# A linear-attention and mixture-of-experts layer on one core: denominators placed directly behind the shared product, shared sums placed behind the reciprocals

## The reference, cut to what matters

```
xn  = layernorm(x)
Q, K, V = heads(xn @ wq.T + bq), heads(xn @ wk.T + bk), heads(xn @ wv.T + bv)   # 16 heads of 32
Q, K = elu(Q) + 1, elu(K) + 1
out = (Q @ (K^T V)) / (Q . sum(K) + 1e-8)          # linear attention, per head
att = out @ wo.T + bo
gate = xn @ W_gate + shared lora + expert loras * w    # up likewise; w from a top-2 router
hidden = silu(gate) * up                               # 1376 wide
ffn = hidden @ W_down + (hidden @ sA_down) @ sB_down / 8 + expert loras of down
result = x + att + ffn
```

## Time and profile before

| | |
|---|---|
| median of 3 runs | 667.39 us |
| the profiled execution's own time | 667.35 us |
| its span, first to last instruction | 665.6 us |
| TensorE busy | 656.5 us (99%) |
| VectorE busy | 376.3 us (57%) |
| ScalarE busy | 259.3 us (39%) |
| GpSimd busy | 127.3 us (19%) |
| granted TensorE clock, mean | 1.000 |

### The profile page before, as it was taken

How to read it: one execution, slowest core, us unless ns; L and a number is a source line. 1 busy time by engine, 2 the same in 40 slices (tenths; PEclk the granted TensorE clock), 3 DMA queues, 4 the chain that set the end, 5 groups by cost and what they waited for, 6 DMA issues and landing times.

```text
span 665.6 us, 10324 instructions
## 1 busy us (share of the span) xinstructions
PE 656.5 (99%) x3557; PEld 544.7 (82%) x3557; DVE 376.3 (57%) x708; ACT 259.3 (39%) x419; POOL 127.3 (19%) x290
## 2 busy tenths in 40 slices
PE   7999999999999999999999999999999999999998
PEld 6889999877777788888888888888888888888886
DVE  6677888779685954433355444355344426534433
ACT  5434444476426323332243333233333324333321
POOL 3565666627336310000000000000000000000000
PEclk9999999999999999999999999999999999999999
DMA  6976665644755679940026000022400001300001
GB/s 216 312 257 210 211 241 196 251 183 158 280 197 212 233 162 3 32 174 0 0 80 247 7 0 0 0 77 76 177 0 0 0 9 70 127 0 0 0 0 63
DMA packets 41642, 74.21 MB, mean 111 GB/s; under 512 B 19392, under 2 KB 20288, under 8 KB 39952
## 3 DMA queue, kind: packets, MB, share of 16 engines
q1 hardware_dynamic: 38672, 64.52, 35.8%
q10 hardware_dynamic: 2736, 9.05, 3.4%
q0 software_dynamic: 208, 0.30, 0.3%
HBM read 52.82 MB, written 21.04 MB: 111 GB/s over the span
## 4 chain that ended last, share of the span: by engine, by line
PE 94%; DVE 4%; DMA 1%; issue 1%; ACT 1%; POOL 0%; DVEq 0%; ACTq 0%; POOLq 0%
PE bank L1268 21%; PE bank L1269 21%; PE bank L1270 21%; PE bank L1514 18%; PE bank L1487 6%; PE bank L1500 2%; PE bank L1498 1%; PE bank L1287 1%; DVE den L1108 1%; PE bank L1299 1%; DMA w_raw<-in_wkT 1%; PE bank L1525 1%; PE bank L1527 1%; PE bank L1308 0%; DVE m_l L903 0%
## 5 line engine op out<-in xcount | busy, mean ns | idle before, releaser
L1268 PE MATMUL bank<-x,up_h 128*128 128x512 f32 (+1 forms) x352 | 137.3, 390 | 0.2 <-DVE x3r L1072 0.2
L1269 PE MATMUL bank<-x,up_h 128*128 128x512 f32 (+1 forms) x352 | 137.1, 390 | 0.0
L1270 PE MATMUL bank<-x,up_l 128*128 128x512 f32 (+1 forms) x352 | 137.1, 389 | 0.0
L1205 DVE TENSOR_TENSOR hf<-bank,silu 128x512 f32<-128x512 f32 x44 | 30.4, 691 | 154.7 <-issue 135.0
L1514 PE MATMUL bank<-dn,hid_h 128*128 128x512 f32 x352 | 108.8, 390 | 0.0
L684 ACT ACTIVATE hid_h<-hf 128x512 fp32r<-128x512 f32 x44 | 27.8, 632 | 142.4 <-DVE hf L1205 142.4
L1268 PEld LDWEIGHTS bank<-x,up_h 128*128 128x128 f32 x352 | 66.1, 188 | 14.4 <-issue 0.7
L1514 PEld LDWEIGHTS bank<-dn,hid_h 128*128 128x128 f32 x352 | 65.9, 188 | 14.5 <-DVE res L1230 0.6
L1270 PEld LDWEIGHTS bank<-x,up_l 128*128 128x128 f32 x352 | 66.1, 188 | 13.8
L1269 PEld LDWEIGHTS bank<-x,up_h 128*128 128x128 f32 x352 | 66.1, 188 | 13.6
L903 DVE TENSOR_TENSOR up_l<-up_raw,up_h 128x1024 fp32r<-128x1024 f32 x44 | 53.9, 1225 | 28.0 <-ACT up_h L684 28.0
(11 more groups left out here) (170 smaller groups left out, 1083.9 us busy)
## 6 DMA issues: line engine op xcount, KB each, us to landing
x<-scr_x SPq DMA_DIRECT2D x7, 2048.0 KB, 8.6
up_raw<-in_ffn_up SPq DMA_DIRECT2D x11, 768.0 KB, 8.2
scr_x<-xt ACTq DMA_DIRECT2D x16, 512.0 KB, 5.1
xin<-in_x SPq DMA_DIRECT2D x16, 256.0 KB, 4.9
scr_z<-zt SPq DMA_DIRECT2D x16, 256.0 KB, 2.1
x3r<-in_x SPq DMA_DIRECT2D x16, 256.0 KB, 3.4
scr_att<-x3r SPq DMA_DIRECT2D x16, 256.0 KB, 3.5
z<-scr_z SPq DMA_DIRECT2D x4, 1024.0 KB, 4.9
```

What stands on the lines that cost most here:

```text
L1205: nc.vector.tensor_tensor(hf[:], ps_u[:], silu[:], ALU.mult).then_inc(h_done, 1)
L1268: nc.tensor.matmul(dst, lh, rh, start=start, stop=False, **kw)
L1269: nc.tensor.matmul(dst, lh, rl, start=False, stop=False, **kw)
L1270: return nc.tensor.matmul(dst, ll, rh, start=False, stop=stop, **kw)
```

## The change

On TensorE the first quarter of `attention` now comes ahead of the shared product, and the denominators stand directly behind it; the other three quarters follow in one piece. The denominators of groups 1 to 3 are written to bank 0, which the even query chunks use, and no longer to bank 2, so the wait for the first shared sum goes. On VectorE the shared sums move from the head of a group to a place behind `reciprocal_lo`, and the second quarter's sum moves from ahead of the reciprocals to behind them (in the last group also behind `split_up_b`).

```diff
-        ps_q, ps_den, ps_exp, ps_att = [bank[0], bank[1]], bank[2], bank[2:6], [bank[6], bank[7]]
+        ps_q, ps_den, ps_exp, ps_att = [bank[0], bank[1]], [bank[2]] + [bank[0]] * (GROUPS - 1), bank[2:6], [bank[6], bank[7]]
...
             def group(g, last=False):
                 if g > 1:
                     queries(g, (1, 2, 3))
-                    shared_down(g, FC - (GROUPS - 2) * SHG if last else SHG)
                 attention(g - 1, (0,))
-                if g == 1:
-                    shared_down(g)
                 if last:
                     split_up_w(0, 0, 1).then_inc(upl_done, 1)
-                attention(g - 1, (1,))
                 reciprocals(g)
                 if last:
                     split_up_b(0, 0).then_inc(upb_done, 1)
+                attention(g - 1, (1,))
                 reciprocal_lo(g)
+                shared_down(g, FC - (GROUPS - 2) * SHG if last else SHG)
                 attention(g - 1, (2, 3))
...
             def denominators(g):
...
-                if g:
-                    pe.wait_ge(dnm_done, (g - 1) * SHG + 1)
                 wait(pe, dene_done, g)
...
             def group3(g, more=True):
                 queries(g, (1, 2, 3))
+                attention(g - 1, (0,))
                 shared_down(g)
-                attention(g - 1, (0, 1))
                 denominators(g)
-                attention(g - 1, (2, 3))
+                attention(g - 1, (1, 2, 3))
                 expand(g)
...
             shared_down(1)
-            attention(0, (1,))
             denominators(1)
-            attention(0, (2, 3))
+            attention(0, (1, 2, 3))
             expand(1)
```

More of the change, by code:

```diff
@@ L1104, in reciprocals @@
                 dve.wait_ge(den_ready, g + 1)
-                nc.vector.tensor_scalar(den[:], ps_den[:], EPS, None, ALU.add).then_inc(dene_done, 1)
+                nc.vector.tensor_scalar(den[:], ps_den[g][:], EPS, None, ALU.add).then_inc(dene_done, 1)
                 dve.wait_ge(dene_done, g + 1)
@@ L1382, in denominators @@
                 pe.wait_ge(q_done, (g + 1) * KD)
-                if g:
-                    pe.wait_ge(dnm_done, (g - 1) * SHG + 1)
                 wait(pe, dene_done, g)
                 for c in range(KD):
-                    last = nc.tensor.matmul(ps_den[c * DK:(c + 1) * DK, :], kcur[:, g // GB, c, :], qf[g % 2][:, c, :], start=True, stop=True)
+                    last = nc.tensor.matmul(ps_den[g][c * DK:(c + 1) * DK, :], kcur[:, g // GB, c, :], qf[g % 2][:, c, :], start=True, stop=True)
                 last.then_inc(den_ready, 1)
```

## The result

| | before | after |
|---|---|---|
| median | 667.17 us (6 runs) | 669.72 us (6 runs) |
| ratio | 1 | 1.0036, 95% interval 1.0026 to 1.0047 |
| span of the profiled execution | 665.6 us | 668.2 us |
| start of the shared product of group 1 | 163.70 | 164.04 |
| from there to `expand` of group 1 | 10.06 | 10.68 |

The change makes the kernel slower by 0.36%. The row "start of the shared product of group 1" is no effect of the change: the first load of weights took 0.3 us longer in this execution. Counted from there, the two traces differ by 62.39 - 60.13 = 2.26 us, all of it ahead of the feed-forward part: +0.62, +0.49 and +1.15 us in the three groups.

What follows compares the result with a forecast made beforehand. TensorE was taken to bound the kernel (94% of the chain). Groups 1 to 3 add 0.53 + 0.46 + 1.23 = 2.22 us to 667.35, giving 669.57, with 0.04 for the median 669.6 us; own range 669.0 to 670.4, 8 in 10 668.1 to 670.7.

Steps and rivals of the forecast that it cites:

- the new wait for `q_done`: Groups 1 and 2: TensorE waits 0.74 and 0.65 us for the last query sum before the denominators; +0.53 and +0.46 us.
- the upper bound: High end for unseen effects: a layout switch after a wait costs another 0.35 us; all groups together +3.27 us, 670.7 us.
- The cover on VectorE: Groups 1 and 2: VectorE finishes 0.3 us ahead of TensorE's `expand`, so nothing waits there; a 0.4 us delay would show.
- D + 9.1: Groups 1 and 2: VectorE's finish with lag, counted from the denominators' start on TensorE; `expand` can start 9.41 us after it.
- The blocks' edges: TensorE: touching blocks need three tiling-mode switches a group instead of four, saving about 0.2 us a group.
- Group 3: Last group: first feed-forward matmul at 225.06 instead of 223.83, +1.23 us, with the old waits of 0.74 us swallowed.
- The stand before quarter 3: Group 3: TensorE needs bank 7, hence VectorE's sum of quarter 1, and starts quarter 3 1.7 us late.
- The second road: Group 3 without the bank 7 wait: VectorE's shared sums and quarter 2 still hold TensorE, at least +1.06 us.
- A: Rival, chance 0.06: faster; `rr` is early, TensorE waits for nobody, 666.1 us.
- B: Rival, chance 0.12: query sums take 0.69 us beside a different bias sum; groups 1 and 2 give -0.4 together, 668.2 us.
- C: Rival, chance 0.10: waits of groups 1 and 2 stay under 0.5 us and cost nothing; only the last group loses, 668.6 us.
- D: Rival, chance 0.03: the 1.7 us stand drops the clock to 1.2 GHz; twelve matmuls cost 2.7 us more, 672.3 us.

Runs made afterwards that it cites:

- e1: New order in groups 1 and 2 only, group 3 in the old order, against the kernel before: 668.58 us (ratio 1.0018).
- e2: New order in group 3 only, groups 1 and 2 in the old order, against the kernel before: 668.48 us (ratio 1.0016).
- e5: The changed kernel without GpSimd's addition of the output bias, which is missing from the result: 668.10 us (ratio 1.0017 to the kernel before).
- e10: The changed kernel with GpSimd's bias for quarter 3 (first group: quarters 2 and 3) added after the last query sum: 668.29 us (ratio 1.0013).
- e8: The changed kernel with VectorE's sum of quarter 1 in group 3 behind the reciprocals but ahead of `split_up_b`: 669.82 us (ratio 1.0036).
- e9: e8 with one of group 3's three shared sums moved into VectorE's idle time before `up_l`: 668.88 us (ratio 1.002).
- e7: The changed kernel with VectorE's sum of quarter 1 in group 3 back ahead of the reciprocals: 672.36 us (ratio 1.008).

## Why the prediction was right

- **Groups 1 and 2, the new wait for `q_done`.** Forecast 0.74 and 0.65 us of standing and +0.53 and +0.46; measured 0.80 and 0.66, and +0.62 and +0.49. e1 and e2 show the loss where it was put, e5 and e10 its cause. The term that was too small is the lag from the query sum to the denominators: 0.10 us taken, 0.26, 0.29 and 0.25 measured (group 1: 163.32 + 1.77 to 165.35). The excess of about 0.16 us is half of the 0.35 us that the upper bound allowed for a switch of layout. A row counts a stand from the modelled end of the shared product, 0.07 us after the moment that the forecast counts from, so 0.80 in the row is 0.87 in the forecast's count. The cover on VectorE held: its shared sums end at D + 8.94, where D + 9.1 was taken.
- **The blocks' edges.** Forecast 0.2 us a group; e5 and e10 show 0.23 and 0.24.
- **Group 3.** Forecast +1.23 us, measured +1.15 (+1.10 alone, in e2). The stand before the denominators was forecast at 0.5 us and measured at 0.64. The stand before quarter 3 is the term that was furthest off: forecast 1.7 us, measured 1.25 in the row and 1.41 by the forecast's count (221.40 + 0.228 to 223.04). TensorE reached quarter 3 0.15 us later, for the longer lag ahead of the denominators; quarter 1's sum ended a little earlier in the stage; and quarter 3 began 0.06 us behind it, where 0.10 was taken. Idle time before `up_l` was forecast at 1.1 (the forecast's own times, 213.93 to 214.96, give 1.03) and measured at 0.95. The second road, at +1.06, was real: e8 takes 0.9 us off the stand before quarter 3 and gains 0.10 us in group 3, and e9 shortens the second road and gains 0.67 more.
- **Nothing behind the hand-over takes it back.** 441.8 us in both traces.
- **The sum.** 2.22 us forecast, 2.26 in the traces and 2.55 between the medians of six runs. That the times agree better than the differences, 669.6 against 669.72, is in part luck: the forecast started from a median of 667.39 us, and three more runs of the kernel before brought it to 667.17. The traces' sum agrees so closely because errors of +0.09, +0.03 and -0.08 us in the three groups cancel. Between the traces' sum and the medians 0.3 us stay open; the first stage alone differs by more than that from one execution to the next.
- **Rivals.** A did not come about: `rr` did come earlier, 222.33 us on the forecast's scale (222.39 forecast, 223.08 before), and TensorE waited elsewhere. B happened in group 2 of the execution of e1 that was traced, and not in that of the changed kernel. C is refuted by e1's median of +1.39 us and by the stands of 0.80 and 0.66 us. D, the clock, did not strike in the trace after, with a stand of 1.25 us, but e7 and e10 show that it was a rival to be taken seriously: e10's stand of 1.78 us is about the length forecast for this kernel (1.7). Its price was 2.7 us by the forecast, which slowed all twelve matmuls, and 1.6 us in e10, where the first three kept their pace.

## What to carry to other kernels

Before a step is moved forward on the bounding engine, find the instruction that completes what it waits for, and look at how long that one takes in its place, beside what another engine runs at that time (here GpSimd's bias sum). In the order of before a quarter of 2.7 us hid a sum stretched by 0.9 to 1.1 us; in the new order nothing did. And a step moved back on a second engine can bring nothing if the bounding engine still needs it before it can go on, least of all if it had filled a gap (here the 0.95 us ahead of `up_l`): count the work ahead of the point where the bounding engine needs the last result, idle time included, in both orders.

## What the runs showed of the hardware

- VectorE's query sum and GpSimd's bias sum hold each other up, and in the two pairs shown the order of their starts decides who pays: 0.02 us in favour of VectorE left it at 0.69 us and made GpSimd's sum 1.81 instead of 1.28 us; 0.23 us in favour of GpSimd made VectorE's 1.60 us (e1 and after). This agrees with the Trainium skill (SBUF — State Buffer, "Who interferes with whom"), by which a VectorE instruction with two SBUF inputs contends with a GpSimd instruction that reads SBUF, and issue order decides who blocks. It does not agree with a block to the very end: the stretched sums of groups 2 and 3 end 0.55 and 0.54 us behind GpSimd, where a sum alone takes 0.69. A kernel at such an edge may have two times: e1 ran from 666.98 to 668.93 us.
- The granted clock of TensorE fell to 0.53 and 0.57 in the stretches behind stands of 2.85 us (e7) and 1.78 us (e10), and stayed at 1.00 behind stands of 1.25 us (after) and 1.80 us (e5). In e10 it fell 0.8 us after work had begun again. The stand of 1.78 us cost 1.6 us more than its length and the one of 2.85 us 1.4 us more. Stands of nearly the same length did it in some executions and not in others; what decides is not shown.
